# Decoder layer in float32 on one core: x also loaded transposed, quantise operands in PSUM, a 17th column for the scale floor, and a shorter root for the key norms

## What is computed

```python
# linear attention, 16 heads of 8
q = elu(x @ Wq + bq) + 1;  k = elu(x @ Wk + bk) + 1;  v = x @ Wv + bv
k = k / sqrt(sum(k * k over the head) + 1e-6)
attn = (q @ k^T) @ v                      # per head, no softmax
ya = layernorm(x + attn @ Wo + bo, 1e-6) * gamma + beta
x1 = layernorm(x + ya)
# cross attention, 16 heads of 64, softmax over 64 context rows
x2 = layernorm(x1 + softmax((x1 Wq)(ctx Wk)^T / 8) (ctx Wv) Wo)
# gated feed-forward; every operand is quantised to FP4 in blocks of 16
def fp4(x):                               # per block of 16
    scale = max(max(|x|) / 6, 1e-12)
    return grid(x / scale) * scale        # grid: 0, .5, 1, 1.5, 2, 3, 4, 6
h = silu(fp4(x2) @ fp4(w_gate)^T) * (fp4(x2) @ fp4(w_up)^T)   # 352 wide
out = layernorm(x2 + fp4(h) @ fp4(w_down)^T)
```

## Time and profile before

| | us |
|---|---|
| median of 3 runs | 439.4 |
| lowest, highest | 437.44, 439.61 |
| the profiled execution | 440.09 |
| its span, first to last instruction | 438.4 |
| PE busy | 375.9 (86%) |
| DVE busy | 358.3 (82%) |
| POOL busy | 296.2 (68%) |
| ACT busy | 254.7 (58%) |
| granted TensorE clock, mean | 0.95 of full |

### The profile page before, as it was taken

How to read it: one execution, slowest core, us unless ns; L and a number is a source line. 1 busy time by engine, 2 the same in 40 slices (tenths; PEclk the granted TensorE clock), 3 DMA queues, 4 the chain that set the end, 5 groups by cost and what they waited for, 6 DMA issues and landing times. The chain is left out here.

```text
span 438.4 us, 8439 instructions
## 1 busy us (share of the span) xinstructions
PE 375.9 (86%) x2089; PEld 269.2 (61%) x2089; DVE 358.3 (82%) x941; ACT 254.7 (58%) x499; POOL 296.2 (68%) x468
## 2 busy tenths in 40 slices
PE   2499797899999999999999999999999989878463
PEld 2487565675757575757575858585848575546243
DVE  1738777669999999999999999999999997865661
ACT  1543646567576767676766666666666655545222
POOL 2003557667888888888888888888888889453031
PEclk9889999999999999999999999999999999988655
DMA  8400000000000000000000000000000000000000
GB/s 245 113 1 13 1 13 0 13 14 0 12 4 24 1 24 0 24 0 24 0 24 0 24 0 24 0 24 0 24 0 24 0 14 1 14 0 12 1 12 25
DMA packets 13684, 8.22 MB, mean 19 GB/s; under 512 B 992, under 2 KB 13280, under 8 KB 13664
## 3 DMA queue, kind: packets, MB, share of 16 engines
q1 hardware_dynamic: 13376, 6.93, 5.6%
q10 hardware_dynamic: 288, 1.05, 0.8%
HBM read 5.88 MB, written 2.10 MB: 18 GB/s over the span
## 5 line engine op out<-in xcount | busy, mean ns | idle before, releaser
L1553 PE MATMUL S<-M,x1T 128*128 (+1 forms) x128 | 60.3, 593 | 0.0
L1593 PE MATMUL F<-w_gu,wT 128*128 128x352 f32 x128 | 48.5, 503 | 7.3 <-DVE h L1144 3.5
L482 POOL TENSOR_TENSOR xo_w<-pe 128x512 f32<-128x512 f32 x32 | 42.9, 1340 | 4.1 <-ACT pe L775 3.1
L470 POOL TENSOR_TENSOR kn<-fk,krn 128x256 f32<-128x256 f32 x16 | 11.1, 692 | 48.0 <-DVE krn L1055 48.0
L1593 PEld LDWEIGHTS F<-w_gu,wT 128*128 128x128 f32 x128 | 22.7, 197 | 33.1 <-DVE h L1144 16.5
L1099 DVE TENSOR_REDUCE smax<-S 128x16 fp32r<-128x1024 f32 x32 | 39.1, 1221 | 4.6 <-PE S L1553 2.4
L507 POOL TENSOR_TENSOR wT<-wT,hs 128x704 f32<-128x704 f32 x16 | 22.2, 1387 | 27.7 <-DVE wT L954 27.7
L491 POOL TENSOR_TENSOR fw_v<-pe,srec 128x1024 f32<-128x1024 f32 x16 | 30.4, 1902 | 9.4 <-DVE srec L1111 9.4
L775 ACT ACTIVATE pe<-S 128x1024 f32<-128x1024 f32 x32 | 32.5, 1015 | 5.0 <-PE S L1561 4.9
L1576 PE MATMUL A<-vo,ctx_rows 128*128 128x128 f32 x256 | 33.0, 285 | 1.2 <-issue 1.2
L1576 PEld LDWEIGHTS A<-vo,ctx_rows 128*128 128x128 f32 x256 | 31.5, 201 | 1.4 <-issue 1.4
(11 more groups left out here) (189 smaller groups left out, 1051.8 us busy)
## 6 DMA issues: line engine op xcount, KB each, us to landing
x_sb<-in_x SPq DMA_DIRECT2D x16, 128.0 KB, 2.1
out<-xv_w SPq DMA_DIRECT2D x16, 128.0 KB, 1.8
xk_w<-in_L_xattn_Wk ACTq DMA_DIRECT2D x1, 512.0 KB, 4.3
ctx_rows<-in_ctx SPq DMA_DIRECT2D x1, 512.0 KB, 7.4
xv_w<-in_L_xattn_Wv ACTq DMA_DIRECT2D x1, 512.0 KB, 6.8
xq_w<-in_L_xattn_Wq SPq DMA_DIRECT2D x1, 512.0 KB, 8.0
xo_w<-in_L_xattn_Wo SPq DMA_DIRECT2D x1, 512.0 KB, 8.5
fw<-in_L_ffn_w_gate SPq DMA_DIRECT2D x3, 64.0 KB, 3.3
```

What stands on the lines that cost most here:

```text
L482: ge.tensor_tensor(phalf[t].rearrange("p (h r) -> p h r", h=HX), p4[:, :, 0, :], p4[:, :, 1, :], ALU.add).then_inc(fold_made, 1)
L1553: last = te.matmul(S[:, half * BANK:half * BANK + BANK], x1T[:, t * P:t * P + P], M[:, HC * half:HC * half + HC, bass.ds(b * R, R)], start ...
L1593: last = te.matmul(bk[:, 0:I], xfT[:, t * P:t * P + P], w_gu[:, m, :], start=True, stop=True)
```

## The change

Seven parts:

1. x comes a second time, transposed, as its own input `x_t`. SP loads it straight into xT once queries, keys and values of the batch before are made. PE's transposes and ACT's copy are gone. The query product now also waits for bank A1 to be left by the quantise.
2. x2 and h have 17 columns per block; the 17th holds 6e-12. The maximum over 17 is never under 6e-12, so the scale step is gone: r = 1/am, v = x * (6 * TIES_DOWN) * r, and POOL multiplies g by am (DVE keeps a scale step for the weights alone). The missing factor 1/6 goes into the weights' last step.
3. The quantise tensors c and r lie in PSUM: for x2 in bank A1, for h in F, and for the last two batches in S.
4. The key norms' root: ACT adds the epsilon (into A1), DVE makes the guess, then two third-order steps: ACT squares y, DVE multiplies by kse (kh), ACT squares kh - 5/3 (kw, in A1), DVE makes the next y = (kw + 20/9) * y. A factor left over goes into head_mask, once.
5. DVE's order: the guess at the end of round i; at the head of round i+1 `k_miss` 0, score sums of tile 1, `k_better` 0, reciprocals, `k_miss` 1, both gate steps of tile 1, `k_better` 1. q_features moves ahead of k_sums. x and h steps shift by one.
6. ACT's order: `q_parts` moves ahead of `keep_x1`; the epsilon ahead of the exponential of tile 1; the square of the guess behind it; the first post-attention norm, the first miss squared, the second norm, the second square, vo, the second miss squared, tanh of tile 1.
7. POOL sets the constants once; its order in the rounds is unchanged, and so is PE's but for part 1.

The diff, cut to its core (the weights' quantise is now a function of its own with the old seven steps, and the order of the end stage shifts with the step numbers):

```diff
+        x2 = sb("x2", [P, T, D // BLK, BLK + 1])
...
+        def h_home(b):
+            w = S if isinstance(b, int) and b >= B - 2 else F
+            return w[:, :].rearrange("p (t n) -> p t n", t=T)[:, :, 0:I], w[:, NK * P:NK * P + NH]
...
+        xc, xr = A1[:, 0:T * P], A1[:, T * P:T * P + NX]
+        kse, kw = A1[:, 0:T * HA], A1[:, T * HA:2 * T * HA]
...
-                sp.wait_ge(xT_made, b)
                 sp.dma_start(x_sb[:, :, :], x[b, :, :].rearrange("(t p) d -> p t d", p=P)).then_inc(x_loaded, 16)
+            def load_xT(b):
+                sp.wait_ge(qT_made, b)
+                sp.wait_ge(kv_made, b)
+                sp.dma_start(xT[:, :], x_t[b, :, :]).then_inc(xT_loaded, 16)
             def store_out(b):
                 sp.wait_ge(out_made, T * b + T)
...
             def iteration(i):
                 if (a := on(i + 1, 0)) is not None:
+                    load_xT(a)
...
+            ge.memset(x2[:, :, :, BLK:BLK + 1], 6.0 * 1e-12).then_inc(pad_made, 1)
+            ge.memset(h[:, :, :, BLK:BLK + 1], 6.0 * 1e-12).then_inc(pad_made, 1)
...
+            ge.tensor_tensor(head_mask[:, :], head_mask[:, :], rsq_scale[:, :], ALU.mult).then_inc(pad_made, 1)
...
-                pool.wait_ge(krn_step, 11 * b + 11)
+                pool.wait_ge(ky_made, 3 * b + 3)
...
-                                 xs[:, :].unsqueeze(2).to_broadcast([P, NX, BLK]), ALU.mult).then_inc(xq_made, 1)
+                                 xam[:, :].unsqueeze(2).to_broadcast([P, NX, BLK]), ALU.mult).then_inc(xq_made, 1)
...
+            def k_sums_eps(b):
+                act.wait_ge(kss_made, b + 1)
+                act.wait_ge(fq_made, b + 1)
+                sc.activation(kse, kss[:, :], ACT.Identity, bias=eps_col[:, :]).then_inc(kse_made, 1)
+            def k_guess_squared(b, n):
+                act.wait_ge(ky_made, 3 * b + n + 1)
+                sc.activation(kyy[:, :], ky[n][:, :], ACT.Square, scale=RSQRT_SCALE ** n).then_inc(kyy_made, 1)
+            def k_miss_squared(b, n):
+                act.wait_ge(kh_made, 2 * b + n + 1)
+                sc.activation(kw, kh[:, :], ACT.Square, bias=third_col[:, :]).then_inc(kw_made, 1)
...
-                sc.activation(xc[:, :], xv[:, :], ACT.Abs, scale=STEP).then_inc(x2_abs, 1)
+                act.wait_ge(x2q_step, 5 * b + 3)
+                sc.activation(xc, xv[:, :], ACT.Abs, scale=STEP).then_inc(x2_abs, 1)
...
+                sc.activation(h_home(b)[0], hv.rearrange("p (t n) -> p t n", t=T), ACT.Abs, scale=STEP).then_inc(h_abs, 1)
...
             def iteration(i):
                 b0, b1, b2, b3, b4, b5 = (on(i, n) for n in range(6))
-                if b0 is not None:
-                    keep_xT(b0)
                 if b4 is not None:
                     x2_magnitudes(b4)
...
                 if b4 is not None:
                     keep_x2(b4)
                     keep_xfT(b4)
+                if b0 is not None:
+                    q_parts(b0)
                 if b2 is not None:
                     keep_x1(b2)
...
                 if b4 is not None:
                     gate_tanh(b4, 0)
+                if b0 is not None:
+                    k_sums_eps(b0)
                 if b2 is not None:
                     softmax_exp(b2, 1)
-                if b1 is not None:
-                    post_attn_norm(b1)
+                if b0 is not None:
+                    k_guess_squared(b0, 0)
+                if b1 is not None:
+                    post_attn_norm(b1, 0)
+                if b0 is not None:
+                    k_miss_squared(b0, 0)
+                if b1 is not None:
+                    post_attn_norm(b1, 1)
+                if b0 is not None:
+                    k_guess_squared(b0, 1)
                 if b2 is not None:
                     keep_vo(b2)
+                if b0 is not None:
+                    k_miss_squared(b0, 1)
                 if b4 is not None:
                     gate_tanh(b4, 1)
...
+            def like(ap, c):
+                return ap if len(c.shape) == 2 else ap.rearrange("p (t n) -> p t n", t=c.shape[1])
+            def quantise(src, n, am, r, v, c, t_, g, step, base, c_made, c_count, first, last):
                 for k in range(first, last):
-                    if k and k != 4:
+                    if k and k != 3:
                         dve.wait_ge(step, base + k)
                     if k == 0:
-                        ve.tensor_reduce(am, blocks(src, n), AX.X, ALU.max,
-                                         apply_absolute_value=True).then_inc(step, 1)
+                        ve.tensor_reduce(am, src, AX.X, ALU.max, apply_absolute_value=True).then_inc(step, 1)
                     elif k == 1:
-                        ve.tensor_scalar(s, am, 1.0 / 6.0, 1e-12, ALU.mult, ALU.max).then_inc(step, 1)
+                        ve.reciprocal(r, am).then_inc(step, 1)
                     elif k == 2:
-                        ve.reciprocal(r, s).then_inc(step, 1)
+                        ve.scalar_tensor_tensor(blocks(v, n), src[:, :, 0:BLK], 6.0 * TIES_DOWN, spread(r, n),
+                                                ALU.mult, ALU.mult).then_inc(step, 1)
                     elif k == 3:
-                        ve.scalar_tensor_tensor(blocks(v, n), blocks(src, n), TIES_DOWN, spread(r, n),
-                                                ALU.mult, ALU.mult).then_inc(step, 1)
+                        dve.wait_ge(c_made, c_count)
+                        ve.scalar_tensor_tensor(like(t_, c), c, STEP * FLOOR, like(v, c), ALU.max,
+                                                ALU.add).then_inc(step, 1)
+                    else:
+                        ve.scalar_tensor_tensor(like(g, c), c, STEP * FLOOR, like(t_, c), ALU.max, ALU.subtract,
+                                                reverse1=True).then_inc(step, 1)
...
-            def k_rsqrt(b, first, last):
-                for k in range(first, last):
-                    if k:
-                        dve.wait_ge(krn_step, 11 * b + k)
-                    else:
-                        dve.wait_ge(kss_made, b + 1)
-                    if k == 0:
-                        ve.tensor_scalar(kse[:, :], kss[:, :], ATTN_EPS, None, ALU.add).then_inc(krn_step, 1)
-                    elif k == 1:
-                        if late(b):
-                            dve.wait_ge(kn_made, b)
-                        ve.tensor_scalar(krn[:, :].bitcast(mybir.dt.int32), kse[:, :].bitcast(mybir.dt.int32),
-                                         -0.5, RSQRT_MAGIC, ALU.mult, ALU.add).then_inc(krn_step, 1)
-                    elif k % 3 == 2:
-                        ve.tensor_tensor(kyy[:, :], krn[:, :], krn[:, :], ALU.mult).then_inc(krn_step, 1)
-                    elif k % 3 == 0:
-                        ve.scalar_tensor_tensor(kxyy[:, :], kyy[:, :], -0.5, kse[:, :], ALU.mult,
-                                                ALU.mult).then_inc(krn_step, 1)
-                    else:
-                        ve.scalar_tensor_tensor(krn[:, :], kxyy[:, :], 1.5, krn[:, :], ALU.add,
-                                                ALU.mult).then_inc(krn_step, 1)
+            def k_guess(b):
+                dve.wait_ge(kse_made, b + 1)
+                ve.tensor_scalar(ky[0][:, :].bitcast(mybir.dt.int32), kse.bitcast(mybir.dt.int32),
+                                 -0.5, RSQRT_MAGIC, ALU.mult, ALU.add).then_inc(ky_made, 1)
+            def k_miss(b, n):
+                dve.wait_ge(kyy_made, 2 * b + n + 1)
+                ve.tensor_tensor(kh[:, :], kyy[:, :], kse, ALU.mult).then_inc(kh_made, 1)
+            def k_better(b, n):
+                dve.wait_ge(kw_made, 2 * b + n + 1)
+                if n == 1 and late(b):
+                    dve.wait_ge(kn_made, b)
+                ve.scalar_tensor_tensor(ky[n + 1][:, :], kw, RSQRT_ADD, ky[n][:, :], ALU.add,
+                                        ALU.mult).then_inc(ky_made, 1)
...
                 if b1 is not None:
-                    k_rsqrt(b1, 4, 5)
-                    k_rsqrt(b1, 5, 6)
-                    k_rsqrt(b1, 6, 7)
-                    k_rsqrt(b1, 7, 8)
-                    k_rsqrt(b1, 8, 9)
-                    k_rsqrt(b1, 9, 10)
-                    k_rsqrt(b1, 10, 11)
+                    k_miss(b1, 0)
                 if b3 is not None:
                     score_sums(b3, 1)
+                if b1 is not None:
+                    k_better(b1, 0)
+                if b3 is not None:
+                    score_reciprocals(b3, 1)
+                if b1 is not None:
+                    k_miss(b1, 1)
                 if b5 is not None:
                     gate_times(b5, 1)
-                if b3 is not None:
-                    score_reciprocals(b3, 1)
                 if b5 is not None:
                     gated(b5, 1)
+                if b1 is not None:
+                    k_better(b1, 1)
...
+                    q_features(b0)
                     k_sums(b0)
...
                 if b0 is not None:
```

(51 more changed lines are left out.)

156 lines of the change are left out of this document (74 added, 82 removed).

## The result

The changed kernel takes 468.3 us (median of 4 runs, which lie between 466.5 and 469.6); the kernel before, run beside it on the same chip, 438.6. The ratio is 1.067, 95% interval 1.063 to 1.071: slower, by 29.7 us. The profiled execution took 467.7 us, its span is 466.0 and its mean granted clock 0.93; before, 438.4 and 0.95.

The account below looks back on a forecast made before the run. DVE was taken to bind the kernel before, PE right behind; afterwards a long cross-engine chain. Span 438.4 + 15.6 (chain) - 3 (end stage) + 14 (clock) = 465, so 466 us; range 447 to 483.

Parts of the forecast that it names:

- the case that had the chance of 0.45: Whole kernel: long queue chain in the steady rounds, with clock falls in some of them; 466 us.
- The long chain: Exponential's end to kv_outer, through the new ACT and DVE orders: 5.90 us against 3.56, round 23.0, +15.6 over 12 rounds.
- the rest of the circle: Round outside that stretch: kv_outer to the next scores 14.95 us, then 2.15 to the exponential's end, kse's 0.15 included.
- The activation on 32 elements: ACT's short squares in the root: taken at 0.25 us each, by the 128-element row, ends 0.10 and 0.47.
- The clock: PE, idle around transposes before kv_outer: half clock costs 2.8 us a fall, five of twelve rounds, +14, ends 0 and +34.
- The relief: DVE's work per round falls from 20.7 to about 16.7 us through root, scale steps and c in PSUM.
- The root: DVE's key-norm root: 2.33 us, three more steps and kse against five steps of 0.19; some 1.8 us less a round.
- No surcharge for PSUM operands: DVE steps reading PSUM: nothing charged; the skill's 65 ns more would be 0.13 a round, 1.6 us in all.
- x transposed at 0: New DMA of transposed x: 0 to 0.5 us in the start, taken as 0.
- Rounds 0 to 3 at 0: First rounds: lacking tanh, hg and h, 1.5 us of the chain, they were put at no added time.
- The end stage, -3: Last stage, without root: DVE loses scale steps and c steps stop meeting POOL; -3 us, ends -1 and -4.
- faster, PE bound: Hand-over before kv_outer: chain under 4.6 us lets DVE's freed 4 us bring the round to 20.4; 422 us, chance 0.13.

Follow-up runs that it names:

- The moves: Three kernels made from the changed kernel: DVE's ky1 put ahead of the score sums, ky2 ahead of the gate products, or both; 445.9, 440.0 and 426.1 us.
- ky2 first: Changed kernel with only DVE's ky2 (k_better 1) put ahead of hg and h of the second tile; 440.0 us, ratio 1.003 to the kernel before.
- both moves: Changed kernel with ky1 put ahead of the score sums and ky2 ahead of hg and h on DVE; 426.1 us, ratio 0.972 to the kernel before.

## Why the prediction was right

Forecast 466.0, measured 468.3, inside the range of 447 to 483, and on the case that had the chance of 0.45. The added 27.6 us of span are +4.4 up to kv_outer of round 3, +25.2 for the twelve rounds, -2.0 in the end stage.

The mechanism was right, but that the sum came within 1.0 us of the measured span (465 and 466.0) is partly luck. The rounds up to 3 cost 4.4 us that the sum put at 0, and the end stage gave 1.0 less than it said; the clock was charged 3.6 us too much and the chain 0.8, and these cancel most of it.

- **The long chain: right.** Forecast 5.90 us, measured 5.91; the round 23.0, measured 22.82 where the clock holds. The 0.2 of difference is in the rest of the circle, 17.1 in the sum (14.95 + 2.15) and 16.9 measured. The moves show the links: ky1 behind the sums and ky2 behind the gates carry the loss. Of the +25.2 it is what the clock leaves, 14.8 (forecast +15.6).
- **The activation on 32 elements**, taken at 0.25: 0.23 without the bias tile and 0.28 with it.
- **The clock: mechanism and place right, price too high.** Six of twelve rounds where five were taken, each low stretch around kv_outer and the products behind it. That the count came so near is no merit of the sum, which gave no reason for five. And a fall cost less: the five long rounds 1.40 to 2.96 us over the plain 22.82, 8.9 together, and the first round 1.5 (19.63 - 18.10 of PE's work), 10.4 in all; the sum had 14 (2.8 each). The step that failed is the price: it was read from one place of the end stage where the low clock held for 5.64 us of PE's work, and only the 25.78 round is like that. In the round behind 163.74, of 24.22, kv_outer took 1.19 and the four products of the scores 2.81 us instead of 0.68 and 1.88, and the next product was back at its usual 0.38.
- **The relief: right in kind, a little large.** DVE 16.7 forecast, 17.26 measured. The steps on c came out as said (0.42 and 0.88 forecast; 0.40 and 0.88, together 1.46 saved for 1.4). Scale steps and c together: 20.70 to 18.59, 2.1 instead of 2.3. The root: 18.59 to 17.26, 1.3 instead of 1.8. The forecast's own terms give more than 1.8: 2.33 + 0.7 for the four steps before the stretch - 0.95 is 2.1. Part of what is missing had gone with the other parts: the root step that met POOL's fold, 1.05 us before, takes 0.72 with the old root in the changed kernel (at 190.72). PE's floor: 20.0 forecast, 20.03 measured.
- **No surcharge for PSUM operands: right.** 188 ns against 191 for steps of the same size. The 65 ns more that the Trainium skill, "VectorE: DVE Perf Modes", section on the TRN2 errata, would give for a PSUM source are not there.
- **x transposed at 0: right in the rounds.** Alone on the kernel before it left the round at 21.66 and the total where it was. Whether PE's 0.84 us counts once DVE is not the bound, no run shows by itself.
- **Rounds 0 to 3 at 0: wrong.** They cost +4.4. The step that failed is "rounds 0 to 3 lack tanh, hg and h": that is so, but the other half of the chain, vo behind the square of ky1, is there from round 2 on, as softmax is. With both moves kv_outer of round 3 comes at 92.62 instead of 95.20, 2.6 of the 4.4. Of the other 1.8, the kernel before with x transposed alone has 0.9 (91.69 against 90.83), and the one with the old root 1.6 (92.39). Their causes weren't tried.
- **The end stage, -3: measured -2.0.** Between the kernels with edits it moved from 84.9 to 88.5 us, with mean clocks from 0.86 to 0.81 in it, so what the steps themselves gave can't be read from it. Most of the 2.0 can be the clock: the place from which the sum read its fall has the same two idle stretches here, 1.47 and 1.16 us, and the clock holds, so the products behind them take 2.02 us instead of 3.76:

```profile
421.20 2.02 PE L1615 MATMUL A<-vo,ctx_rows 128*128 128x128 f32 x16 [1.16 <-issue]
```

- **The rival "faster, PE bound"**, 422 us if the chain stays under 4.6 us: that case was built by the moves. ky2 first has a chain of 4.55 and a round of 21.47, a little under the 21.66 of before, so 4.6 is about where the chain stops costing. But the round doesn't drop to 20.4 there, as the rival had it: it goes down with the chain, to 20.37 at 3.44, and only then is the total 424.4.

## What to carry to other kernels

When a step is spread over a second engine to relieve a full one, write down which instruction stands ahead of each new link in both queues; here a root of steps of 0.2 to 0.3 us each, queued behind a 1.3 us fold, a 1.0 us copy and two gate products, cost 43 us, and moving three of its steps won all of it back. Put a link of a cross-engine chain where its input arrives, ahead of work whose input comes later. Ask also whether the engine relieved is still the bound after the other parts: here the old root, left alone, is as fast as the new one in its best order.

## What the runs showed of the hardware

- From round 4 on and up to the end stage, the clock fell only in kernels where both idle stretches of PE (1.23 and 1.44 us) stood with nothing but transposes between them. With the first shortened to 0.13 and the second at 1.86, or with 1.23 and none, it stayed at 1.00 in all rounds from 5 on; with both filled by products that nothing reads, too, from where they were filled. In the first rounds it also fell with idle ahead of the transposes alone (1.02 and 1.73 us in round 3, with ky2 first and in the changed kernel), so this pair is not the only case.
- In rounds with the same idle stretches the clock fell or held within one execution (five and six of the eleven full ones), and a fall cost from 1.40 to 2.96 us. What decides either is open.
- A short POOL instruction on 2 elements took 0.84 instead of 0.20 us beside a DVE step with two SBUF operands, and a DVE step on 256 columns took a mean of 1.24 us instead of 0.40 with one of them in PSUM: the contention is paid on both sides.
